# Output weights' operands in chunks of 128 columns, and output products spread 3, 4, 3, 4 over a set of four heads

## What is computed

```python
xn = layernorm(x)                                   # 4 x 512 tokens, 1024 wide
qkv = xn @ w_qkv                                    # 32 heads, 8 groups of K and V, D = 128
p = softmax(q k / sqrt(D) - slope * sqrt(distance)) # causal, 4 heads to a K/V group
attn = (p @ v) @ w_o                                # w_o: 4096 x 1024
ffn = xn @ W.T + b + routed_lora(xn)
out = x + attn + ffn
```

## Time and profile before

| | us |
|---|---|
| median of 3 runs | 2562.22 (2561.83 to 2563.93) |
| the profiled execution | 2561.72 |
| its span, first to last instruction | 2559.9 |
| PE busy | 2400.9 (94%) |
| DVE, ACT, POOL busy | 1606.0, 1395.7, 664.6 |

### The profile page before, as it was taken

How to read it: one execution, slowest core, us unless ns; L and a number is a source line. 1 busy time by engine, 2 the same in 40 slices (tenths; PEclk the granted TensorE clock), 3 DMA queues, 4 the chain that set the end, 5 groups by cost and what they waited for, 6 DMA issues and landing times.

```text
span 2559.9 us, 35267 instructions
## 1 busy us (share of the span) xinstructions
PE 2400.9 (94%) x11616; PEld 2005.3 (78%) x11616; DVE 1606.0 (63%) x3265; ACT 1395.7 (55%) x3219; POOL 664.6 (26%) x901
## 2 busy tenths in 40 slices
PE   5999998998599999889968999999999999999999
PEld 4787876777577887677757888888888888888887
DVE  6657466656575636656656666666666666666665
ACT  4432244334452313434436777777777777777774
POOL 3211000000222100000003444444444444444444
PEclk9999999999899999999989999999999999999999
DMA  4546386788535547687785677685776758577653
GB/s 149 182 132 222 136 275 229 256 262 282 188 116 168 193 159 228 238 282 250 259 307 216 238 246 255 216 289 198 251 255 247 255 206 281 207 266 251 233 195 140
DMA packets 197044, 573.41 MB, mean 224 GB/s; under 512 B 17961, under 2 KB 91833, under 8 KB 180736
## 3 DMA queue, kind: packets, MB, share of 16 engines
q1 hardware_dynamic: 164896, 451.83, 51.2%
q0 software_dynamic: 31968, 119.33, 13.4%
HBM read 335.68 MB, written 235.41 MB: 223 GB/s over the span
## 4 chain that ended last, share of the span: by engine, by line
PE 68%; DVE 12%; DMA 8%; ACT 5%; issue 4%; SPq 2%; POOL 1%; DVEq 0%; ACTq 0%; POOLq 0%
PE ps L693 21%; PE ps L694 20%; PE ps L695 20%; DMA wp_raw<-w_o 6%; PE ps L889 5%; DVE w_lo L1198 2%; DVE wp L1198 2%; ACT res_hi L957 1%; DVE res_a L1288 1%; ACT w_hi L957 1%; DMA wo_s<-wp 1%; SPq L424 1%; SPq L412 1%; DVE raw L1277 1%; DVE raw L1280 1%
## 5 line engine op out<-in xcount | busy, mean ns | idle before, releaser
L693 PE MATMUL ps<-x_hi,w_hi 128*128 128x512 f32 x1120 | 451.0, 403 | 65.5 <-DVE w_lo L1198 54.6
L1482 DVE TENSOR_TENSOR acc<-ps,acc 128x512 f32<-128x512 f32 x448 | 298.2, 688 | 311.2 <-issue 284.1
L694 PE MATMUL ps<-x_lo,w_hi 128*128 128x512 f32 x1120 | 445.1, 397 | 0.0
L695 PE MATMUL ps<-x_hi,w_lo 128*128 128x512 f32 x1120 | 444.4, 397 | 0.0
L957 ACT ACTIVATE w_hi<-raw 128x1024 fp32r<-128x1024 f32 x196 | 205.8, 1053 | 339.8 <-PE ps L695 225.3
L693 PE MATMUL ps<-wo,op_hi 128*128 128x512 f32 x896 | 361.6, 404 | 2.4 <-POOL op_lo L675 2.4
L1097 ACT ACTIVATE probs<-probs,neg_max 128x512 f32<-128x512 f32 (+3 forms) x512 | 284.1, 567 | 145.5 <-DVE neg_max L1447 145.5
L694 PE MATMUL ps<-wo,op_hi 128*128 128x512 f32 x896 | 351.5, 392 | 0.0
L695 PE MATMUL ps<-wo,op_lo 128*128 128x512 f32 x896 | 350.6, 391 | 0.0
L1198 DVE TENSOR_TENSOR w_lo<-raw,w_hi 128x1024 fp32r<-128x1024 f32 x196 | 238.8, 1222 | 175.8 <-ACT w_hi L957 175.4
L693 PEld LDWEIGHTS ps<-x_hi,w_hi 128*128 128x128 f32 x1120 | 215.6, 192 | 126.1 <-DVE w_lo L1198 81.6
(11 more groups left out here) (164 smaller groups left out, 4689.8 us busy)
## 6 DMA issues: line engine op xcount, KB each, us to landing
raw<-w_all SPq DMA_DIRECT2D x70, 1024.0 KB, 7.1
q<-qk_s SPq DMA_DIRECT2D x128, 512.0 KB, 3.9
acc<-acc_s SPq DMA_DIRECT2D x128, 512.0 KB, 5.4
wo_s<-wp SPq DMA_DIRECT2D x224, 256.0 KB, 5.2
wo<-wo_s SPq DMA_DIRECT2D x56, 1024.0 KB, 7.3
acc_s<-acc SPq DMA_DIRECT2D x112, 512.0 KB, 8.3
qk_s<-res_hi POOLq DMA_DIRECT2D x40, 1024.0 KB, 4.7
qk_s<-res_a POOLq DMA_DIRECT2D x20, 1024.0 KB, 7.3
```

The source lines that it names most:

```text
L693: pe.matmul(to, st_hi, mv_hi, start=start, stop=False, skip_group_check=True)
L694: pe.matmul(to, st_hi, mv_lo, start=False, stop=False, skip_group_check=True)
L695: return pe.matmul(to, st_lo, mv_hi, start=False, stop=stop, skip_group_check=True)
L1482: nc.vector.tensor_tensor(to, fill[f % 2][:, :], to, ALU.add).then_inc(s_acc, 1)
```

## The change

Instead of quarters of 256 columns, whose seven operands are made one by one, `w_o` is cut on the host into 64 chunks of 128 columns that hold all four blocks side by side (a21, a11, a12, a22). A chunk is one load of 256 KB into one of three places, and two halves of work: half 0 copies and subtracts the three plain blocks (384 columns) and makes the four sums in place, half 1 copies and subtracts the four sums (512 columns). Each half has one place for its result, stored with one DMA (384 and 512 KB). `STEP_HALVES` says how many halves are done in each half step; all query matrices have 16 now, Q3 too. `wo` and `wo_s` keep high and low parts in alternating blocks of 128 columns, so an output product reads its moving operand as four blocks. The first group's seven operands are loaded one a unit, in units 1 to 7. `SHARES` becomes 3, 4, 3, 4: three products in even units, four in odd ones.

```diff
-SHARES = (range(0, 4), range(4, 7), range(7, 11), range(11, 14))
+SHARES = (range(0, 3), range(3, 7), range(7, 10), range(10, 14))
...
-JOBS = QUARTERS * STEPS
-WO_ORDER = (6, 1, 0, 4, 2, 5, 3)
-STEP_JOBS = (3, 5, 4, 5, 5, 4, 4)
-LAST_JOBS = (3, 5, 4, 5, 4, 2, 0)
-SLOTS = 4
+CHUNK = 128
+CHUNKS = 8 * KV_HEADS
+STEP_HALVES = (0, 1, 1, 1, 1, 1, 2, 2, 2, 2, 1, 1, 1, 0)
+WP_PLACES = 3
+WO_ORDER = (0, 1, 6, 4, 3, 5, 2)
+WO_HALVES = (slice(0, 3), slice(3, 7))
...
-        wp_raw = [at(f"wp_raw{i}", (192 + i) * K, [P, 256]) for i in range(4)]
-        wp = at("wp", 196 * K, [P, SLOTS, 2, 256], F32R)
+        wp_raw = [at(f"wp_raw{i}", (192 + 2 * i) * K, [P, 4, CHUNK]) for i in range(WP_PLACES)]
+        wp = [at("wp_blocks", 198 * K, [P, 3, 2, CHUNK], F32R), at("wp_sums", 201 * K, [P, 4, 2, CHUNK], F32R)]
...
-        wo = [at(f"wo{i}", place_ * K, [P, 2, 1024], F32R) for i, place_ in enumerate((*range(86, 158, 8), 34, 42))]
+        wo = [at(f"wo{i}", place_ * K, [P, 8, 2, CHUNK], F32R) for i, place_ in enumerate((*range(86, 158, 8), 34, 42))]
...
-        wo_s = nc.dram_tensor("wo_s", (KV_HEADS, STEPS, P, 2, 1024), F32).ap()
+        wo_s = nc.dram_tensor("wo_s", (KV_HEADS, STEPS, P, 8, 2, CHUNK), F32).ap()
...
-        def jobs(pr, m, st, part=None):
+        def jobs(pr, m, st, part):
...
+            first = CHUNKS // PAIRS * 2 * pr + sum(STEP_HALVES) * QUERIES[m] + sum(STEP_HALVES[:2 * st + part])
+            return [(i // 2, i % 2) for i in range(first, first + STEP_HALVES[2 * st + part])]
...
-            def quarter(c, i):
...
+            def chunk(c):
+
+                sp.dma_start(wp_raw[c % WP_PLACES][:, :, :], w_o[c]).then_inc(s_wp_raw[c % WP_PLACES], 16)
+
+            def operands_out(pr, m, st, part):
+
+                if (m, st, part) == (Q0, 0, 0):
                     sp.wait_ge(s_bank, 4 * (number(pr, FFN, STEPS - 1) + 1))
...
+                    for i in range(WP_PLACES):
+                        chunk(pr * CHUNKS // PAIRS + i)
+                for c, half in jobs(pr, m, st, part):
+                    sp.wait_ge(s_wp_lo, 2 * c + half + 1)
+                    sp.dma_start(wo_s[c // 8, WO_HALVES[half], :, c % 8].rearrange("k p l c -> p k l c"),
+                                 wp[half][:, :, :, :].bitcast(F32)).then_inc(s_wp_out[half], 16)
+                    if half and c % (CHUNKS // PAIRS) + WP_PLACES < CHUNKS // PAIRS:
+                        chunk(c + WP_PLACES)
...
             def out_weights(n):
 
-                if n in (1, 2):
-                    if n == 1:
-                        sp.wait_ge(s_bank, 4 * TOTAL)
-                        operands_are_out(JOBS)
-                    for step in (range(0, 4), range(4, STEPS))[n - 1]:
-                        out_operand(0, step)
+                if n == 1:
+                    sp.wait_ge(s_bank, 4 * TOTAL)
+                    operands_are_out(CHUNKS)
+                if n in range(1, STEPS + 1):
+                    out_operand(0, n - 1)
...
                 for kt in range(2):
-                    cols = slice(kt * 512, (kt + 1) * 512)
+                    four = slice(4 * kt, 4 * kt + 4)
                     last = product(fill[f % 2][:, :], (op_hi[:, k, kt, :], op_lo[k][:, kt, :]),
-                                   (wo[home][:, 0, cols], wo[home][:, 1, cols]), kt == 0 and k in STARTS, kt == 1)
+                                   (wo[home][:, four, 0, :], wo[home][:, four, 1, :]), kt == 0 and k in STARTS, kt == 1)
...
+            def job(c, half):
+
+                if c:
+                    act.wait_ge(s_wp_out[half], 16 * c)
+                if half:
+                    act.wait_ge(s_wp_sum, 4 * (c + 1))
                 else:
-                    act.wait_ge(s_wp_sum, 4 * c + (4, 2, 5, 3).index(step) + 1)
-                high(wp[:, j % SLOTS, 0], wp_source(step), s_wp_hi)
+                    act.wait_ge(s_wp_raw[c % WP_PLACES], 16 * (c // WP_PLACES + 1))
+                high(wp[half][:, :, 0, :], wp_raw[c % WP_PLACES][:, 1 - half:4, :], s_wp_hi)
...
+            def job(c, half):
+
+                dve.wait_ge(s_wp_hi, 2 * c + half + 1)
+                if half:
+                    dve.wait_ge(s_wp_sum, 4 * (c + 1))
+                low(wp[half][:, :, 1, :], wp_raw[c % WP_PLACES][:, 1 - half:4, :], wp[half][:, :, 0, :], s_wp_lo)
+                if half:
                     return
...
+                a21, a11, a12, a22 = (wp_raw[c % WP_PLACES][:, i, :] for i in range(4))
                 nc.vector.tensor_tensor(a21, a11, a21, ALU.subtract).then_inc(s_wp_sum, 1)
...
+def chunks(matrix):
+
+    by = matrix.reshape(GROUPS, 2, 2, P, 2, 4, CHUNK).transpose(0, 2, 5, 3, 4, 1, 6)
+    four = np.stack([by[..., half, pair, :] for half, pair in ((1, 0), (0, 0), (0, 1), (1, 1))], axis=4)
+    return four.reshape(CHUNKS, P, 4, CHUNK)
...
-        "w_o": f(L0_attn_w_o),
+        "w_o": f(chunks(np.asarray(L0_attn_w_o))),
```

More of the change, by code:

```diff
@@ L115, in block_program @@
         d_lo = at("d_lo", 192 * K + 10624, [P, 512], F32R)
[L117 to L119 removed]
+        rest = 205 * K
+        wp_raw = [at(f"wp_raw{i}", (192 + 2 * i) * K, [P, 4, CHUNK]) for i in range(WP_PLACES)]
+        wp = [at("wp_blocks", 198 * K, [P, 3, 2, CHUNK], F32R), at("wp_sums", 201 * K, [P, 4, 2, CHUNK], F32R)]
         ident = at("ident", rest, [P, P])
@@ L231, in block_program @@
         s_v = [sem(f"s_v{i}") for i in range(2)]
-        s_wp_raw = [sem(f"s_wp_raw{i}") for i in range(4)]
+        s_wp_raw = [sem(f"s_wp_raw{i}") for i in range(WP_PLACES)]
         s_wp_sum = sem("s_wp_sum")
@@ L235, in block_program @@
         s_wp_lo = sem("s_wp_lo")
-        s_wp_out = [sem(f"s_wp_out{i}") for i in range(SLOTS)]
+        s_wp_out = [sem(f"s_wp_out{i}") for i in range(2)]
         s_wo = [sem(f"s_wo{i}") for i in range(STEPS)]
@@ L405, in weights @@
                 sp.dma_start(raw[i][:, :], w_all[m, i]).then_inc(s_raw[i], 16)
-            def quarter(c, i):
[L409 to L416, removed]
-                    sp.wait_ge(s_bank, 4 * (number(pr, FFN, STEPS - 1) + 1))
[L418 to L428, removed]
@@ L430, in operands_are_out @@
             def operands_are_out(count):
-                for i in range(SLOTS):
-                    sp.wait_ge(s_wp_out[i], 16 * len(range(i, count, SLOTS)))
+                for half in range(2):
+                    sp.wait_ge(s_wp_out[half], 16 * count)
             tokens(0, 0)
@@ L1163, in _ @@
                         later_operand(pr, m, st, 1)
-                        for j in jobs(pr, m, st, 0):
-                            job(j)
+                        for chunk in jobs(pr, m, st, 0):
+                            job(*chunk)
                         weights(n + 1, 1)
@@ L1168, in _ @@
                         ahead(pr, m, st)
-                        for j in jobs(pr, m, st, 1):
-                            job(j)
+                        for chunk in jobs(pr, m, st, 1):
+                            job(*chunk)
                 leave(number(pr, MATRICES - 1, STEPS - 1))
@@ L1482, in add_fill @@
                 nc.vector.tensor_tensor(to, fill[f % 2][:, :], to, ALU.add).then_inc(s_acc, 1)
[L1484 to L1491 removed]
+            def job(c, half):
[4 more added lines that the diff above has]
+                if half:
                     return
[L1493 to L1494 removed]
+                a21, a11, a12, a22 = (wp_raw[c % WP_PLACES][:, i, :] for i in range(4))
                 nc.vector.tensor_tensor(a21, a11, a21, ALU.subtract).then_inc(s_wp_sum, 1)
[L1496 removed]
+                dve.wait_ge(s_wp_lo, 2 * c + 1)
                 dve.wait_ge(s_wp_sum, 4 * c + 1)
```

25 lines of the change are left out of this document (6 added, 19 removed).

## The result

The kernel after takes **2591.47 us** (median of 4, 2590.15 to 2593.22), the kernel before 2563.01 (2561.83 to 2563.93) beside it: ratio 1.0112 [1.0096, 1.0128], 28 us slower. I had said 2521 and a range up to 2562. The two profiled spans, 2559.9 and 2590.7, differ by 30.8.

A forecast was written before the change was run, and what follows sets the result against it. TensorE was taken as the bound, except for 99.3 us lost mainly to late weight loads in the query matrices. From 2561.7 us, -75 + 6 - 6 + 34 = -41 gave 2521 us, range 2486 to 2562.

The forecast's parts named there:

- The loads' wait: Query matrices: ScalarE's 180.4 us of waits for loads of raw output weights taken as gone with three places.
- One place per half: Query matrices: a half's copy waits for its previous store; of 99.3 us lost 24 stay, a gain of 75.
- the 79.1 us a matrix: Query matrices: 55.0 us of VectorE and ScalarE chain plus 24.1 for three store rounds, against TensorE's 76.1.
- L = 6.2: Steps 3 and 4: assumed landing time in us of an operand store, making a round 8.0 us.
- the fast rival: Query matrices: stores land in 3.6 us, the gain is 95 and the total 2501 us; chance 0.18.
- Rival 2: Query matrices: store wait replaces load wait, L 9.0, gain only 8, total 2588 us, slower; chance 0.11.
- Products 3, 4, 3, 4: Attention: in 61 odd units the fourth product waits for VectorE's add behind inverses, 0.56 us each, +34.
- The last matrix no longer eased: Between the pairs: Q3's steps 5 and 6 now hold halves, lengthening TensorE's wait for VectorE, +6 us.
- First unit's q: Start of attention: k, q, v, dist issued some 8.4 us later, behind the last operand store, +6 us.
- Third unit's q: Start of attention: q stands behind 1 or 2 MB of wo, not 4, so TensorE's wait goes, -12 us.
- Four blocks of 128 as moving operand: Output products: reading the moving operand in four blocks costs 0 to 9 us, taken as 0.

The follow-up runs named there:

- e10: e6 plus, behind each short store, another in SP's queue making up its bytes that nobody waits for until the pair's end: 2576.60 us.
- e6: Kernel after with only 16 of 128 partitions of each operand half stored (48 and 64 KB for 384 and 512 KB): 2537.30 us.
- e13: e10 with the extra stores that nobody waits for issued by POOL in its own queue, not by SP: 2581.91 us.
- e4: Kernel after with the halves of the output weights' chunks spread evenly over the 14 half steps: 2586.51 us.
- e5: Kernel after with the stores of the output weights' operands issued by POOL, not by SP: 2587.19 us.
- e7: Kernel after with SP's last store of operands behind the first unit's loads of k, q, v and dist: 2583.46 us.
- e11: e9 and e4 together, results' wait and sums' loads a unit later, first unit's loads ahead of the stores of steps 5 and 6: 2531.24 us.
- e3: Kernel after with the first group's seven 1 MB loads in units 1 and 2 again: 2599.66 us.
- e1: Kernel after with the old spread of products, 4, 3, 4, 3: 2551.88 us.
- e9: Kernel after, spread 3, 4, 3, 4 kept, with VectorE's add of the second product ahead of the reciprocals: 2549.96 us.

## Why the prediction was wrong, step by step

**The loads' wait** was to go and went, 180.4 us to none.

**One place per half, -75 for -21.** This is the step that failed: the 79.1 us a matrix. It counted three rounds of the wait, within steps 3 and 4, with one landing L = 6.2 for both halves, and took everything else at full speed. Q1 and Q2 took 86 to 89 us. Three things in it were wrong.
1. *The bytes stayed.* I costed a matrix by the chain of DVE and ACT alone. The change moves nearly as many bytes: 247 GB/s x 94.4 us before in Q1, 263 x 87.8 after, 23 MB each. In 79.1 us that would be 294 GB/s; no single matrix with the whole bytes got past 274 (e10's Q1, 377.9 to 462.2 us). The prediction used this ("the same bytes must go in 10% less time") as an argument against the fast rival only. That the bytes cost time is shown by e6, e10 and e13: 54 us with fewer of them, 15 or 10 with short stores and the whole bytes. That a rate sets the limit is not: the 79 us stretches above had 288 and 291 GB/s, 2 and 1% under 294. By what path the bytes slow a matrix, by the landings of the stores, of the 1 MB loads, or both, stays open.
2. *Landing isn't a property of a store.* Sums land in 3.7, blocks in 6.4, by what is issued ahead; e10 has 6.0 for 48 KB. The round that I had not counted, from step 2's blocks to the first of step 3, is the longest: its store takes 9.7 us to land, and its waits are 65 of 140.5 us. An estimate from the fit of the Trainium skill ("DMA: Bandwidth & Descriptors", the anatomy of one SWDGE DMA) is 3.2 us for 512 KB and 2.9 for 384 KB. The page gives it for GpSimd's path, and these stores go by SP's queue; the trace has 3.7 for the first and 2.5 to 9.7 for the second, by its place, so the measurement decides. No run issues step 2's store ahead of the 1 MB load, and what that would give is not known.
3. *The cover was taken twice.* Moving the wait (e4, e5) changed the six matrices by 1.6 us and by nothing, so cutting rounds bought what another wait took.

Part of what a matrix loses isn't idle time: in Q1 after, PE is busy 81.5 us for 338 matmuls that take 76.6 at full clock, at a mean granted clock of 0.94, between the levels of 1.2 and 2.4 GHz; in e10 the same stretch has 1.00. Over both windows of the kernel after PE is idle for 52 us, and its matmuls are in flight 26 us longer than the 598 that they need at full clock. So the gains of e10 and e6 hold some of the clock, too.

Rival 2 had the sign and, at 2588, nearly the time, and it too had the wrong account: it put 8 us on the matrices where they gave 21, and missed 9 at q and 8 in the odd units. That its number came so near is luck: these errors nearly cancel.

**Products 3, 4, 3, 4: +34 for +42.** Mechanism, place and count held (61 waits, 26.3 us); the term was under-sized by 0.15 us a unit. The timeline of one odd unit, PE and the add on DVE:

```profile
2039.87 0.39 PE L680 MATMUL ps<-wo,op_lo 128*128 128x512 f32 x1
2040.69 0.47 PE L678 MATMUL ps<-wo,op_hi 128*128 128x512 f32 x1 [0.43 <-DVE acc L1466]
2041.00 0.39 PE L679 MATMUL ps<-wo,op_hi 128*128 128x512 f32 x1
...
2039.85 1.29 DVE L1466 TENSOR_TENSOR acc<-ps,acc 128x512 f32<-128x512 f32 x2
```

The product could have started at 2039.87 + 0.23 = 2040.10 and started at 2040.69: 0.59, where the row says 0.43, since a matmul's record runs 0.39 us but the next starts 0.23 behind it. The add is over at 2039.85 + 0.69 = 2040.54; PE follows 0.15 later, which I had left out. The restart, 0.31 to the next matmul in place of 0.23, costs 0.08 more (I had 0.11). Together 0.67, of 0.71 measured.

**The last matrix no longer eased: +6, in another place.** Q3 of the first pair takes 91.8 us up to its last step, after 84.4; I had looked for it between the pairs, where PE's waits are 10.29 in place of 11.26. The window of the matrices holds it, so it is part of the 21.

**First unit's q: +6 for +15.** The order in SP's queue was right. The last store went out at 1291.91, and that k and q would then take 8.9 us to land was in my bounds; but PE came there at 1282.3, 21 earlier than before (1303.4), and q's landing only 6 earlier (1301.9 for 1308.0), and that I did not carry over: what a stretch gives back is not a gain if the next thing awaited hangs on SP. e7 takes 8.8 us off this wait and e11 13.4.

**Third unit's q: -12 for -5.** The wait fell by 9.0, and uncovered the one for k of the second set. "Needed more than a unit after its issue" was true of wo; of SP's next wait I did not ask. e3 puts the edit of these loads at 8.2.

**Four blocks of 128 as moving operand: 0.** Right: e1's attention stretch is whole and e9's window from 1388 to 2501 holds 6008 matmuls, as 6006 before.

## What to carry to other kernels

Where a change takes a wait away, look for the next one behind it. For each place that is written again, follow the transfer that frees it through its queue, with what is issued ahead of it: the same 384 KB landed here in 2.5 or in 9.7 us, and the median of 6.4 tells neither. Work out, too, the rate that the same bytes would need in the shorter time. If no stretch of that length has reached it, that is a warning, though not yet a cause. And where two engines share two banks, see which add each product waits for, and what that add stands behind in its engine's order: here moving one line was worth 1.6%.

## What the runs showed that I had not expected

- A store of 48 KB took 6.0 us to land (median of 23) with full traffic in its queue and 7.0 with the extra traffic in the other queue only; with the traffic at 208 GB/s in place of 269, 4.5. In one place of the matrix, behind the 1 MB load, it took 8.5 even then.
- Moving the operands' stores to POOL's queue made SP's 1 MB loads slower, 6.4 to 7.4 us, not faster.
- A wait that the list gives as 0.43 us costs PE 0.67: 0.59 of late start and 0.08 of restart.
